# Post-norm decoder block on one core: in six of eight units, weighing ahead of the second scores and dividing ahead of the copy of the maxima

## The reference

```python
q = proj(Wq, bq); k = proj(Wk, bk); v = proj(Wv, bv)
scores = jnp.einsum('bqhd,bkhd->bhqk', q, k) / scale
attn = jax.nn.softmax(scores + bias[None, :, None, :], axis=-1)
out = jnp.einsum('bhqk,bkhd->bqhd', attn, v).reshape(B, L, D)
return jnp.einsum('bld,ed->ble', out, Wo) + bo
...
x = _layernorm(x + _L0_attn_ref(x, ...))
x = _layernorm(x + _L0_xattn_ref(ctx_1024, ctx_1024, x, mask_Bx1x1xS2_fk0, ...))
x = _layernorm(x + _L0_ffn_ref(x, ...))
```

## Time and profile before

| What | us |
|---|---|
| median of 3 runs (lowest to highest) | 1310.53 (1307.91 to 1312.72) |
| the profiled execution's own time | 1307.59 |
| its span in the profile | 1305.7 |
| attention's full passes, first to last | 86.8 to 730 |
| experts' stage | about 760 to 1306 |
| TensorE busy over the span | 1084.3 (83%) |
| VectorE busy over the span | 972.5 (74%) |
| ScalarE, GpSimd busy over the span | 567.5 (43%), 487.6 (37%) |

### The profile page before, as it was taken

How to read it: one execution, slowest core, us unless ns; L and a number is a source line. 1 busy time by engine, 2 the same in 40 slices (tenths; PEclk the granted TensorE clock), 3 DMA queues, 4 the chain that set the end, 5 groups by cost and what they waited for, 6 DMA issues and landing times. The chain is left out here.

```text
span 1305.7 us, 32355 instructions
## 1 busy us (share of the span) xinstructions
PE 1084.3 (83%) x9894; PEld 772.1 (59%) x9895; DVE 972.5 (74%) x2213; ACT 567.5 (43%) x1025; POOL 487.6 (37%) x603
## 2 busy tenths in 40 slices
PE   3778988999898898989888671889999999999970
PEld 2446666666665566656665441767777777777650
DVE  1668888888886889888888653667777777777754
ACT  1435555555554666676666330222232332323325
POOL 1233343334433534545653573122223223222224
PEclk7899999999999999999999755999999999999995
DMA  8577867786657688789887586652222222222228
GB/s 186 133 179 172 182 142 182 178 207 126 175 111 164 152 243 240 171 232 267 249 221 214 165 283 222 223 164 44 42 44 41 45 43 42 43 42 42 44 29 262
DMA packets 153670, 194.03 MB, mean 149 GB/s; under 512 B 30636, under 2 KB 133948, under 8 KB 149323
## 3 DMA queue, kind: packets, MB, share of 16 engines
q1 hardware_dynamic: 139144, 174.67, 50.8%
q0 software_dynamic: 13296, 17.83, 8.1%
q10 hardware_dynamic: 1152, 0.53, 0.2%
HBM read 122.63 MB, written 66.16 MB: 145 GB/s over the span
## 5 line engine op out<-in xcount | busy, mean ns | idle before, releaser
L1418 PE MATMUL HB<-xhi,W 128*128 128x128 f16 x2272 | 291.8, 221 | 21.8 <-issue 15.7
L1418 PEld LDWEIGHTS HB<-xhi,W 128*128 x2272 | 202.0, 98 | 66.2 <-issue 48.5
L1623 POOL DMA_INDIRECT d_sums<-ysc,tok x71 | 110.8, 1561 | 323.7 <-ACT ysc L1484 213.3
L1418 PE MATMUL HB<-xlo,W 128*128 128x128 f16 x1136 | 224.9, 220 | 0.0
L844 DVE TENSOR_REDUCE peaks<-SA 128x4 f32<-128x1024 f32 x128 | 156.6, 1224 | 66.3 <-PE SA L696 65.8
L1134 ACT ACTIVATE PT<-SB 128x1024 f32<-128x1024 f32 x128 | 131.1, 1024 | 120.7 <-PE SB L744 118.4
L1418 PEld LDWEIGHTS HB<-xlo,W 128*128 x1136 | 111.9, 99 | 49.7
L1540 DVE SCALAR_TENSOR_TENSOR hlo<-HB,hhi 128x512 f16<-128x512 f32 x142 | 98.2, 692 | 55.4 <-ACT hhi L1476 51.7
L1476 ACT ACTIVATE hhi<-HB 128x512 f16<-128x512 f32 x142 | 84.2, 593 | 118.4 <-DVE HB L1532 118.2
L1484 ACT ACTIVATE ysc<-yb,wv 128x256 f32<-128x256 f32 x71 | 36.1, 508 | 193.3 <-DVE yb L1564 184.1
L1532 DVE SCALAR_TENSOR_TENSOR HB<-HB,SC,b1c 128x512 f32<-128x512 f32 x142 | 107.1, 754 | 15.1 <-PE HB L1418 9.5
(11 more groups left out here) (205 smaller groups left out, 2371.6 us busy)
## 6 DMA issues: line engine op xcount, KB each, us to landing
wst<-in_w SPq DMA_DIRECT2D x32, 1024.0 KB, 10.3
d_w<-w SPq DMA_DIRECT2D x16, 1024.0 KB, 8.3
W<-d_w SPq DMA_DIRECT2D x16, 1024.0 KB, 7.4
k_stack<-d_k SPq DMA_DIRECT2D x96, 128.0 KB
XB<-d_rows SPq DMA_DIRECT2D x65, 130.0 KB
d_q<-q_part SPq DMA_DIRECT2D x16, 384.0 KB, 5.9
d_k<-k_part SPq DMA_DIRECT2D x16, 384.0 KB, 2.7
q_stack<-d_q SPq DMA_DIRECT2D x16, 384.0 KB, 4.6
```

The costliest lines, as they stand in the source:

```text
L1418: mm = pe.matmul(out, w.rearrange("p e n -> p (e n)"), x[n % 2][:, k, :], start=(k == 0 and half == 0 and x is xhi), stop=(k == KT - 1 and ...
L1623: pool.indirect_dma_start(YS, bass.IndirectOffsetOnAxis(ap=tok[n % 6][:, 0:1], axis=0), ysc[n % 2][:, :], None, compute_op=ALU.add).then_i ...
```

## The change

`KEYED_FIRST` holds units 0 and 1, which keep the old order. In units 2 to 7 TensorE weighs before second scores 0 instead of behind them, and VectorE divides before the spread instead of behind it. No instruction is added or removed, and the waits go with their instructions.

```diff
+    KEYED_FIRST = (0, 1)
...
                 scores(u, 1, i)
-                keyed(u, 0, i)
-                weigh(u, i)
+                if u in KEYED_FIRST:
+                    keyed(u, 0, i)
+                    weigh(u, i)
+                else:
+                    weigh(u, i)
+                    keyed(u, 0, i)
                 gap(u, 1, i)
                 keyed(u, 1, i)
...
-            if on(b):
-                wait(dve, f"mcopy{c}", NG * b + g + 1)
-                dve.tensor_copy(stack[q][PROD:PROD + AUX, ...], mts[...]...).then_inc(sem(f"aux{c}"), 1)
+            def spread():
+                if on(b):
+                    wait(dve, f"mcopy{c}", NG * b + g + 1)
+                    dve.tensor_copy(stack[q][PROD:PROD + AUX, ...], mts[...]...).then_inc(sem(f"aux{c}"), 1)
+
+            if u in KEYED_FIRST:
+                spread()
             if on(b3):
                 chain.wait()
...
                                   ).then_inc(sem(f"norm{c3}"), 1)
+            if u not in KEYED_FIRST:
+                spread()
```

More of the change, by code:

```diff
@@ L866, in spread_and_divide @@
                 chain.put(dve.reciprocal(rc[:, :, :], turned[:, :, :, HD]))
-            if on(b):
-                wait(dve, f"mcopy{c}", NG * b + g + 1)
-                dve.tensor_copy(stack[q][PROD:PROD + AUX, GH * g:GH * g + GH, :],
-                                mts[0:AUX, :].unsqueeze(1).to_broadcast([AUX, GH, L])
-                                ).then_inc(sem(f"aux{c}"), 1)
+            def spread():
+                if on(b):
+                    wait(dve, f"mcopy{c}", NG * b + g + 1)
+                    dve.tensor_copy(stack[q][PROD:PROD + AUX, GH * g:GH * g + GH, :],
+                                    mts[0:AUX, :].unsqueeze(1).to_broadcast([AUX, GH, L])
+                                    ).then_inc(sem(f"aux{c}"), 1)
+            if u in KEYED_FIRST:
+                spread()
             if on(b3):
```

## The result

The changed kernel took 1331.74 us (median of 4 runs, 1329.0 to 1332.86) where the kernel before took 1311.62 us (1307.91 to 1313.28): a ratio of 1.0151, 95% interval 1.0128 to 1.0174. It is slower by 20 us; I had forecast 15 us and a range that ended at 1331. The profiled execution has a span of 1329.7 us, 24.0 us above the one before; that is 4 us more than the medians differ, because the profiled execution of the kernel before was its shortest.

The account below looks back on a forecast made before the run. TensorE and VectorE were both nearly full, with hand-overs setting the pace. 8 x 1.09 + 7 x 0.95 = 15.4 us, taken as +15 us on the 1310.53 us median, gave 1325 us; range 1311 to 1331.

Parts of the forecast that it names:

- the waits simply go: Rival for units 2, 4, 5 and 6: exponentials ready in time, 0.74 us saved a pass, 1299 us; chance 0.10.
- nothing change: Rival for the whole pass: losses and gains cancel or find slack, 0.3 us or less either way, about 1311 us; chance 0.16.
- Unit 2 (+0.51 us forecast): Unit 2: second scores 1 wait for exponentials the weighing no longer covers, +0.51 us a pass, +0.37 us in later passes.
- The chain of 1.78 us: Start of second scores 0 through exponentials to start of second scores 1, read uncovered in unit 1: 1.78 us.
- The collision in unit 4: Unit 4: VectorE's moved spread falls into GpSimd's last K operation, +0.26 us a pass; +0.02 us without collision.
- Unit 5 and the turn of unit 7: Unit 5 saves 0.13 us; the turn in unit 7 waits for the later copy of AV, +0.45 us a pass.
- at most 0.1 us is added to the turn of unit 0, and I take nothing: Unit 7: item R waits for VectorE's already late bank reading, so the new order there was counted as costing nothing.
- the chain of 2.06 us: From second scores of unit 6 through exponentials and the copy of AV to the turn in unit 7: 2.06 us.
- the second kind of pass: Passes 9 to 15, where the spread ends later: 0.95 us each, against 1.09 us for passes 1 to 8.
- The term for pass 0: Passes 0 and 16, holding half of the units, add about 1 us; seam passes may hide as much.
- Its waits for transfers are three: TensorE has three transfer waits, one of 15.1 us, so a shift in one pass carries into the next.
- The third rival: Unit 2: moved spread starts behind a GpSimd operation, second scores 1 another 0.54 us later, 1329 to 1333 us; chance 0.12.

Follow-up runs that it names:

- u2_both: Changed kernel with unit 2 back in the old order and ScalarE's first projection part and AV copy ahead of the exponentials in units 3 to 7: ratio 1.0006 to the kernel before.
- part_first: Changed kernel with ScalarE writing the first bfloat16 part of a projection ahead of the exponentials in units 2 to 7: ratio 1.0153 to the kernel before.
- u2_back: Changed kernel with unit 2 back in the old order on both TensorE and VectorE: ratio 1.0038 to the kernel before.
- cross_avs: Kernel before with the change in units 5 to 7 alone and ScalarE's copy of AV ahead of the exponentials there: ratio 0.9930 to the kernel before.
- avs_first: Changed kernel with ScalarE's copy of AV ahead of the exponentials in units 2 to 7: ratio 1.0103 to the kernel before.
- odd_only: Kernel before with the change in units 3, 5 and 7 alone, K's first part and AV copy ahead of the exponentials there: ratio 0.9986 to the kernel before.

## Why the prediction was too low

**Direction and mechanism.** Right. The change saves waits for VectorE and pays more for exponentials, and the loss is carried from pass to pass. The rivals that had the waits simply go, or nothing change, fell.

**Unit 2 (+0.51 us forecast).** Measured 0.53 us by undoing it. The chain of 1.78 us, read in unit 1, held to 0.01 us. The saving was a bit larger, since the weighing follows its division by 0.06 us and not by 0.14: in pass 5 second scores 1 stand 9.83 us behind Qc where they stood 9.38 us, 0.45 us later.

**The collision in unit 4 (+0.26 us, or 0.02 without it).** It happened where the sum put it; second scores 0 started 21.0 us behind Qc, where the sum had 20.93. Undoing it gave 0.36 us, where the two bounds differ by 0.24 us. The undersized part is 0.1 us.

**Unit 5 and the turn of unit 7 (-0.13 and +0.45 us).** The turn's share measured 0.36 us. What units 3 and 5 save is left over from the total: 1.29 - 0.53 - 0.36 - 0.36 - 0.29 = -0.25 us. No run undid it alone, but two readings fit: `u2_both` lies 0.29 us under the kernel before, and in pass 5 item V of unit 5 starts 3.29 us behind second scores 1 of unit 4 where it started 3.58 us behind them. So the sum's 0.13 us was too small by half.

**The step that failed in the pass** is the sentence on unit 7, "at most 0.1 us is added to the turn of unit 0, and I take nothing". I had looked at item R and at VectorE's reading, which both come late, and not at the copy of AV. In the kernel before, 2.53 us lay between the second scores of unit 7 and the turn of unit 0, 0.47 us more than the chain of 2.06 us. In the new order the second scores stand 3.15 us behind the turn of unit 7 instead of 2.48 us, 0.67 us later, and that is more than the slack. Measured by undoing it: 0.29 us a pass, 4 us over the kernel. The chain was already in the prediction for unit 6; it was not applied to the next unit.

**The steps that failed in the sum** are the terms around the first loop. By the two profiled executions:

| Term | sum | measured |
|---|---|---|
| up to Qc of pass 1 | about 1 us, with pass 16 | 2.8 us |
| passes 1 to 8 | 8 x 1.09 = 8.7 us | 10.2 us |
| passes 9 to 15 | 7 x 0.95 = 6.7 us | 11.2 us |

The largest miss is the second kind of pass. The sum made it cheaper than the first by 0.14 us, from one wait. In passes 12 and 13 this holds: they lost 1.17 us each, 0.12 us less than the 1.29 us of the first loop. But passes 9 to 11 lost 1.62, 1.91 and 1.54 us (9 to 13 together 7.4 us: 225.87 against 218.46 us). There VectorE, late by the long spread of unit 4, starts L965 together with an operation of GpSimd, as in pass 9 (the operation takes 0.74 us at this place of the kernel before):

```profile
462.71 1.82 DVE L965 SCALAR_TENSOR_TENSOR w<-wst,SC,w 128x512 f16<-128x512 f32 x1
462.72 1.26 POOL L1253 TENSOR_TENSOR x1bo<-x1s,rows_b 128x512 f32<-128x512 f32 x1
```

The same stands in passes 10 and 11 and not in 12 and 13, nor in `part_first`, where the spread of unit 4 is short. The clock has no part in this: it is 1.00 over each of passes 9 to 13 in both kernels. No run undid this collision alone.

The term for pass 0 is the sentence "Passes 0 and 16 ... add up to about 1 us, and the seam passes with other work may hide as much". The projection Qc of pass 1 starts 2.8 us later (82.27 against 79.47 us). In pass 0 unit 3 has no item Oc yet, and its second scores 1 wait 1.20 us for exponentials; in units 2 and 4 of that pass TensorE runs at the lower clock, and second scores 0 take 1.04 us there instead of 0.60.

And the clock took part at the ends, which no step of the prediction considered. Passes 1 and 14 of the kernel before, and then of the changed kernel:

```profile
79.47:120.39 40.92, 34.80 (x291) 23.15 (x291) 33.88 (x72) 21.11 (x35) 15.61 (x19) 1.00 0.76 177
...
645.79:687.88 42.09, 37.11 (x318) 25.33 (x317) 36.50 (x82) 27.27 (x46) 22.70 (x27) 1.00 0.90 258
```
```profile
82.27:126.70 44.43, 36.51 (x290) 24.16 (x290) 34.80 (x72) 20.94 (x35) 15.85 (x19) 0.96 0.73 168
...
666.17:711.03 44.86, 38.58 (x319) 26.00 (x317) 36.40 (x82) 27.59 (x46) 23.08 (x27) 0.96 0.88 252
```

They grew by 3.51 and 2.77 us, the granted clock falling from 1.00 to 0.96 in both, while pass 2, in which it rose from 0.96 to 1.00, became 0.40 us shorter (44.55 to 44.15 us). An estimate from these rows: 0.04 of a pass of 44.4 us is 1.8 us, so about half of what pass 1 lost, and more than half for pass 14, is the clock, and pass 2 got as much back. Added up: 2.8 us before the first mark, 3.1 us in passes 1 and 2, 6.5 in 3 to 7, 0.6 in pass 8, 7.4 in 9 to 13, 3.8 in 14 and 15 make 24.2 us up to Qc of pass 16, against 24.0 us between the spans. The experts' stage is as long as before, as forecast.

**A reading that was incomplete.** "Its waits for transfers are three" is true of `k_stack` alone. TensorE also waited 7.6 us in six waits for `cq_stack` and 5.0 us for `xT`. All these waits fell from 33.4 us to 28.6 us, so the transfers did swallow a part of the lateness, some 5 us.

**The third rival** (the moved spread loses to GpSimd in unit 2) gave 1329 to 1333 us, and the time fell there, but its mechanism did not occur: the spread started at 310.52, 0.05 us ahead of GpSimd's operation, and took 0.42 us; GpSimd's took 1.39 us instead of 1.16. SBUF — State Buffer in the Trainium skill, section "Who interferes with whom", says of VectorE's two-port modes that whoever issues first gets the shared pair for the whole instruction and the other is blocked. For the spread the trace agrees, and both orders now stand in this case: ahead by 0.05 us in unit 2, behind by 0.03 us in unit 4. A time inside a rival's range is no evidence for the rival.

**Left open.** Why `u2_back` and `cross_avs` gain more in the whole than in passes 3 to 7, why `part_first` gains nothing in the whole, and what the collisions of L965 in passes 9 to 11 are worth by themselves.

## What to carry to other kernels

When two pieces of work change places on one engine, ask what the second one was covering: here the weighing hid ScalarE's exponentials from TensorE, and 0.24 us of saved waits bought 0.75 us of new ones. Then follow every result that stands behind the moved dependence on the next engine's queue, in every unit and the next pass too; reordering that queue as well (`avs_first`) gave back half of the first loop's loss. The one kernel that was faster, by 0.7% with an interval from 0.3 to 1.1%, has the change only where the cover is not needed, and the copy moved along (`cross_avs`). A pass that repeats can be costed to a tenth of a us, but the first pass, the other kind of loop and the seams need a reading of their own: pass 0 and the second kind of pass made 6 of the 8 us that the three terms were short.

## What the hardware showed beyond that

For the spread, 0.03 to 0.05 us settled who was held up: a spread that started 0.03 us behind a GpSimd operation took 1.41 us, and one that started 0.05 us ahead of it 0.42 us, with the GpSimd operation longer by 0.23 us. L965, a scalar_tensor_tensor with both inputs in SBUF, did not go by that: in pass 9 it started 0.01 us ahead of GpSimd's operation and was the one held up, 1.82 us instead of 0.74, while GpSimd's took its 1.26 us. So small a lead may lie within what the trace tells apart.

In a busy stretch a wait of TensorE of 1.93 us was followed by matmuls at the lower clock, 1.03 us for a group of 0.60 us; 46 us later a wait of 1.94 us at the same place was not. An edit that shortens every pass of one loop was worth nothing that could be measured in the whole (`part_first`, `odd_only`).
